# Graph layers on one core: where the second bisection bracket opens, who awaits the first layer step's stores, and the order in which the edge stage opens

## What is computed

```python
def L0(X, S):                                  # two steps s = 0, 1
    S = S + eye(n)
    Rf = S / S.sum(axis=1)[:, None]; Rb = S / S.sum(axis=0)[:, None]
    Xf, Xb, Xa, Z = X, X, X, 0
    for s in range(2):
        logits = (Xa @ W1) @ W2 @ (Xa @ W3).T
        # per row: keep the largest entries whose softmax adds up to 0.9, softmax over these
        A = nucleus(logits, 0.9)
        Xf, Xb, Xa = Rf @ Xf, Rb @ Xb, A @ Xa
        Z = Z + Xf @ U1[s] + Xb @ U2[s] + Xa @ U3[s]
    return layernorm(X + Z) * gamma + beta

def L1(x, adj):                                # the edge stage
    node_att = softmax(x @ node_w, axis=0)
    h = x @ edge_w
    e = where(adj > 0, h @ h.T, NEG_BIG)
    return adj * (node_att * softmax(e, axis=1)) @ (x @ weight) + bias

h = relu(layernorm(x)); x = x + L0(h, adj)
h = relu(layernorm(x)); x = x + L1(h, adj)
```

## Time and profile before

| | |
|---|---|
| median of 3 runs | 3840.46 us |
| the profiled execution | 3846.29 us, span 3844.5 us, mean granted PE clock 0.888 |
| DVE busy | 3540.4 us (92%) |
| ACT busy | 3104.4 us (81%) |
| PE busy | 3004.2 us (78%), weight load 2102.5 us |
| POOL busy | 358.5 us (9%) |
| first layer step, from its first to its last row | 54.95 to 1604.38 us |
| second layer step | 1609.59 to 3140.8 us |
| edge stage | from 3297.82 us |

### The profile page before, as it was taken

The page is one execution under the profiler, slowest core; times in us unless marked ns, Lnnn a source line. Parts: engine busy times, 40 slices in busy tenths (PEclk is TensorE's granted clock), DMA queues, the critical chain, the costliest instruction groups (busy, mean ns, idle before and its releaser), DMA issues. The chain is left out here.

```text
span 3844.5 us, 41925 instructions
## 1 busy us (share of the span) xinstructions
PE 3004.2 (78%) x14148; PEld 2102.5 (55%) x14148; DVE 3540.4 (92%) x4636; ACT 3104.4 (81%) x4477; POOL 358.5 (9%) x417
## 2 busy tenths in 40 slices
PE   6568887787878776648978888796978536799999
PEld 4456666575656654414544545363544425577777
DVE  6999999999999999699999999999999969577776
ACT  6999999999999999399899999999999913233333
POOL 3000000000000000000000000000000017234443
PEclk9689889898988988869989999898989768899999
DMA  2112121222222220211111111111111025122221
GB/s 90 63 54 87 63 97 54 92 67 79 80 67 87 68 78 15 109 56 49 52 35 47 35 57 32 45 42 40 53 35 47 7 80 193 46 104 103 98 91 50
DMA packets 108904, 254.28 MB, mean 66 GB/s; under 512 B 11984, under 2 KB 47888, under 8 KB 105360
## 3 DMA queue, kind: packets, MB, share of 16 engines
q1 hardware_dynamic: 82768, 217.76, 17.6%
q10 hardware_dynamic: 25920, 33.83, 2.5%
HBM read 217.47 MB, written 34.08 MB: 65 GB/s over the span
## 5 line engine op out<-in xcount | busy, mean ns | idle before, releaser
L691 DVE SCALAR_TENSOR_TENSOR s_dump<-s_rows,s_mid 128x3327 bf16<-128x3327 f32 x608 | 2238.3, 3681 | 1.0 <-issue 0.6
L637 ACT ACTIVATE s_adump<-s_rows,s_mid 128x3327 int8<-128x3327 f32 x324 | 995.1, 3071 | 10.5
L643 ACT ACTIVATE s_adump<-s_rows,s_mid 128x3327 int8<-128x3327 f32 x324 | 990.8, 3058 | 0.0
L899 PE MATMUL bank<-x,s_slab 128*128 128x512 f32 x1352 | 629.3, 609 | 0.0
L876 PE MATMUL bank<-kh,qs 128*128 128x512 f16 (+1 forms) x364 | 146.4, 402 | 365.5 <-DVE s_rows L670 354.9
L899 PEld LDWEIGHTS bank<-x,s_slab 128*128 128x128 f32 x1352 | 265.4, 197 | 277.4 <-issue 265.6
L943 PE MATMUL bank<-hb,s_wT 128*128 128x256 f32 x1352 | 355.9, 408 | 70.7 <-ACT s_wT L515 70.7
L943 PE MATMUL bank<-xab,s_wT 128*128 128x256 f32 x1352 | 351.0, 405 | 71.8 <-ACT s_wT L515 71.6
L1334 ACT ACTIVATE e_wh<-bank 128x512 f16<-128x512 f32 (+1 forms) x182 | 102.4, 565 | 343.2 <-PE bank L1438 343.2
L932 PE MATMUL bank<-ident,s_rows 128*128 128x128 f32 x1352 | 229.7, 297 | 190.5 <-DVE s_rows L745 189.4
L899 PE MATMUL bank<-hb,s_slab 128*128 128x257 f32 x1352 | 358.1, 407 | 0.0
(11 more groups left out here) (176 smaller groups left out, 4806.1 us busy)
## 6 DMA issues: line engine op xcount, KB each, us to landing
s_slab<-adjT_dram SPq DMA_DIRECT2D x104, 448.0 KB, 3.9
e_adj<-adjR_dram SPq DMA_DIRECT2D x26, 1664.0 KB, 7.0
s_slab<-adjT_dram SPq DMA_DIRECT2D x104, 384.0 KB, 3.7
strip<-adjR_dram SPq DMA_DIRECT2D x52, 448.0 KB, 3.5
strip<-adjR_dram SPq DMA_DIRECT2D x52, 384.0 KB, 3.3
su_d<-s_su_out ACTq DMA_DIRECT2D x26, 256.0 KB, 2.0
zu_d<-s_zu_out ACTq DMA_DIRECT2D x26, 256.0 KB, 2.0
sx_d<-s_sx_out ACTq DMA_DIRECT2D x26, 256.0 KB, 2.0
```

Of the source, the lines that this page charges most:

```text
L637: nc.scalar.activation(adump[:], row(g, r), ACT.Sign, bias=st(mid, g, 2), accum_out=cnt[:]).then_inc(S["a_eval"], 1)
L643: nc.scalar.activation(adump[:], row(g, r), ACT.Relu, bias=st(mid, g, 2), accum_out=gap[:]).then_inc(S["a_eval"], 1)
L691: nc.vector.scalar_tensor_tensor(out=dump[:], in0=row(g, r), scalar=st(mid, g, r), in1=row(g, r), op0=ALU.is_gt, op1=ALU.mult, accum_out=s ...
L899: ins = nc.tensor.matmul(acc, slab[:, i % NSLAB, j - PIECES[p], :], s_op[:, j, 0:SN], start=False, stop=(j == NT - 1))
```

## The change

Four edits in one kernel.

1. In `layer_step`, `begin(g, 1)` no longer stands ahead of the first pass of role 0 but between its `judge` and the first pass of role 1, in each of the groups 0 to 7 of both steps.
2. The three semaphores of the stores belong to the level above the first step (`kept_in`), are not cleared behind it, and ACT doesn't wait for them at its end. In the second step SP waits for them ahead of its first load, and DVE ahead of its memset. POOL's clears behind the first step become 49.
3. In `phase_edges`, `penalty(1)` stands behind `penalty(0)`, ahead of the first takes.
4. DVE's multiplication of row 0 by the adjacency stands behind the third take of row 1 (`EARLY = 3`), not ahead of the first.

```diff
@@ program
             later = [sb0(n, [P, NPAD], F16) for n in ("qs1", "kh1", "kl1")]
+            kept_in = {n: l0.enter_context(nc.semaphore("s0_" + n)) for n in ("xt_stored", "su_stored", "zu_stored")}
@@ layer_step
+            S.update(env["kept_in"])
...
             if s == 1:
+                for n in ("xt_stored", "su_stored", "zu_stored"):
+                    sp.wait_ge(env["kept_in"][n], 16 * NT)
                 for p in range(NPIECE):
...
-            if s == 0:
-                for n in ("xt_stored", "su_stored", "zu_stored"):
-                    act.wait_ge(S[n], 16 * NT)
-            else:
+            if s == 1:
                 act.wait_ge(S["sx_stored"], 16 * NT)
...
+            if s == 1:
+                for n in ("xt_stored", "su_stored", "zu_stored"):
+                    dve.wait_ge(env["kept_in"][n], 16 * NT)
             nc.vector.memset(rows[:, :, N:NPAD], 0.0).then_inc(S["rows_zero"], 1)
...
             for g in range(LAST):
-                for r in range(2):
-                    begin(g, r)
+                begin(g, 0)
                 for it in range(BISECT):
                     for r in range(2):
+                        if it == 0 and r == 1:
+                            begin(g, 1)
                         evaluate(g, it, r)
@@ phase_edges
+    EARLY = 3
...
             penalty(0)
+            penalty(1)
             dve.wait_ge(na["cut"], 1)
...
             nc.vector.tensor_scalar(col[:, 2:3], col[:, 1:2], -1.0, None, ALU.mult).then_inc(na["shift"], 1)
-            penalty(1)
-            dve.wait_ge(S["exp_done"], 1)
-            nc.vector.tensor_tensor(em[:, 0], em[:, 0], adj[:, 0], ALU.mult).then_inc(S["w_ready"], 1)
             for ch in range(NCH):
+                if ch == EARLY:
+                    dve.wait_ge(S["exp_done"], 1)
+                    nc.vector.tensor_tensor(em[:, 0], em[:, 0], adj[:, 0], ALU.mult).then_inc(S["w_ready"], 1)
                 take(1, ch)
             highest(1)
```

More of the change, by code:

```diff
@@ L405, in layer_step @@
             S.update({n: sem(tag + n) for n in (
-                "col_done", "csum_done", "rsum_ready", "rinv_ready", "turned", "xt_ready", "xt_stored", "su_done", "su_taken", "su_stored",
-                "zu_done", "zu_taken", "zu_stored", "qk_done", "k_high", "q_high", "qk_low", "q_kept")})
+                "col_done", "csum_done", "rsum_ready", "rinv_ready", "turned", "xt_ready", "su_done", "su_taken",
+                "zu_done", "zu_taken", "qk_done", "k_high", "q_high", "qk_low", "q_kept")})
         else:
```

## The result

The changed kernel takes 3831.22 us (median of 14 runs, 3828.26 to 3835.75), the kernel before 3841.47 us (14 runs, 3840.18 to 3843.55). The ratio is 0.9972, 95% interval 0.9965 to 0.9979: 10.8 us less by the ratio, with an interval of 8 to 13 us. The forecast was 3831.1 us, by a sum of 9.4 us.

The account below looks back on a forecast made before the run. DVE bounds the layer steps, PE the edge stage. Bracket 2.7, stores 1.0 and edges 5.7 sum to 9.4 us off the profiled 3846.29, less 5.8 to the runs' median: 3831.1 us, range 3827.5 to 3834.5.

Parts of the forecast that it names:

- The bracket: Layer steps, role 1's opening moved: two waits saved (6.40 us), pair's price 3.84 lost, 0.14 back at heads; net +2.7 us.
- 16 prices of 0.24: Layer steps: in all 16 groups the pair between judge and second pass costs 0.24 us, 3.84 us lost in total.
- The rival that the pair is nearly free: Layer steps: the pair costs only 0.12 us, so the bracket gives 4.6 us and the time is 3829.2; chance 0.15.
- what the sum would have been by the sentence of the Trainium skill: Layer steps: with no extra semaphore cost, the bracket's sum would be its upper bound, +4.6 us instead of +2.7.
- The stores: Boundary between the layer steps: store wait and three clears leave DVE's gap, +1.0 us, between 0.5 and 1.4.
- The rival that the boundary doesn't hang on the store: Boundary between the steps: only three clears go and three waits come, time 3832.1 us; chance 0.05.
- The edges: Edge stage's opening: row 1's maximum starts 5.7 us earlier and everything behind shifts with it; bounds 4.8 to 6.6.
- my upper bound: Edge stage's opening: if PE returns at the high clock and stays there, the gain is 6.6 us.
- The rival in which the penalty isn't made up: Edges, row 0: the penalty's 1.8 us are lost, sum 7.6, time 3832.9; chance 0.16 together with a take-over loss.
- The rival of a long stretch at the lower clock: Edge stage: a 60 us stretch at granted clock 0.58 would cost PE 25 us, time 3856; chance 0.04.

Follow-up runs that it names:

- the price alone: Kernel before, with role 1's opening moved behind the judge in groups 1 to 7 only, group 0 as before: 3843.61 us, ratio 1.0003.
- few_clears: Changed kernel, with semaphores of first stage, first layer step and edge stage never cleared, their clear blocks and barriers left out: 3820.33 us, ratio 0.9949.
- third_penalty: Changed kernel plus role 1's opening ahead of role 0's judge, those three stages' clears dropped, third penalty row behind row 1's second take: 3816.13 us.
- b_only: Kernel before, with the edit of the stores alone: 3841.64 us, ratio 0.9997.
- takes_only: Kernel before, with three takes ahead of the edges' multiplication, second penalty left behind row 0's maximum: 3837.59 us, ratio 0.999.

## Why the prediction was right

**The bracket.** All steps held: the first passes start 3.2 us earlier, the second passes 0.37 us behind the judge, ACT follows at the take-over because PE, and so ACT, hung on DVE's `qs` instruction (PE restarts 0.44 us behind its start in both kernels, and the wait at the take-over stayed 0.97 us), and 1.5 and 1.4 us per step arrive at the ninth group. Forecast +2.7, by the stamps +2.9. The forecast counted 16 prices of 0.24; the one of the fourth group was not paid. The rival that the pair is nearly free falls by the changed kernel's own stamps, and the price alone shows it again without the gain. With it falls what the sum would have been by the sentence of the Trainium skill, VectorE: DVE Perf Modes, section The DRAIN you can't avoid, that "the semaphore costs nothing extra here". For these instructions of 0.14 us the trace doesn't agree with it: the next one starts 0.06 us later if it needs nothing of them (241.86, 241.92), and 0.18 if it does (241.44, 241.62). No run here tests it for long instructions.

What the forecast didn't have is that a part of that price in the second step may be no loss. DVE waits there for PE's logits in the middle of some groups: 3.0 us before, 3.2, 2.8, 2.4, 2.1, 1.8, 1.6, 1.4 and 1.0 us in the eight other traces without the pair behind the judge, and 0, 0, 0.4 and 1.7 us in the four with it. Where DVE would have waited anyway, being later costs nothing. These waits also differ between kernels that are alike there, so how much of the difference is the pair's and how much is PE's clock stays open.

**The stores.** Forecast +1.0 (0.5 to 1.4), measured 0.8: 4.47 to 4.49 us in four traces, against 5.29. The trace also holds POOL's clears themselves, which the views leave out, and they divide the gap. From DVE's last end to the first clear it was 0.95 us and is 0.25; from there to the last clear's end 3.95 and 3.74; from there to the memset 0.39 and 0.50. So the store was worth 0.7 us, three clears 0.2, and the three waits ahead of the memset cost 0.1. The rival that the boundary doesn't hang on the store falls by the first of the three.

The size of one part was off: I took a clear at 0.06 us from gaps with 25 and 30 of them, and for 49 that line gives 3.85 us where the gap is 4.48. A clear starts 0.071 us behind the one before it, at every boundary. But in the row of 49, as in the 52 of before, one of them starts 0.36 us behind the one before it, 0.3 us late. That pause, 0.2 us from the clear's size and the 0.1 us of the waits make up the difference. What causes the pause no run shows; without the clears of the first two boundaries it stands among the 30 ahead of the edge stage, whose gap is 3.02 us there.

**The edges.** Forecast +5.7 (4.8 to 6.6), measured 5.4 by the changed kernel's trace, but by two errors that cancel. I let PE come back at the lower clock for the third chunk; it came back at the higher one after 1.94 us of idling, and again after 2.80, so row 1's maximum gained my upper bound, 6.6. And I let everything behind it shift unchanged; PE's next restart fell into a longer stretch at the lower clock than before, and that gave back 1.2 us. That the two nearly cancel is luck. The traces with both edits, without few_clears and third_penalty, need 45.5, 45.5, 47.6, 47.6 and 47.7 us from memset to row 2's maximum, those without either edit 52.8 to 53.4. The term is thus 5 to 8 us, by where the lower clock fell. In few_clears the granted clock was at the lower level until 5.7 us behind the memset (3.0 to 3.2 us in the other five), row 0's maximum came 1 us later than in the others, two more such stretches followed, and it needed 50.1. The rival in which the penalty isn't made up falls: row 0's maximum came 0.06 us later, not 1.8. The rival of a long stretch at the lower clock didn't happen: 1.00 from 3338 us on.

**The sum** of what the change did by its own places is 9.1 us, forecast 9.4, measured by the ratio 10.8 (8 to 13). That the forecast time, 3831.1 us, meets the median within 0.1 us is luck in part: it starts from the median of three runs, 3840.46, and the longer series has 3841.47 for the same kernel.

## What to carry to other kernels

A wait taken off one place by moving an instruction is paid at each place to which it is moved: count its repetitions, and look for a spot where it stands under another wait (here, ahead of the judge instead of behind it, the same two instructions went from 0.24 us to nothing). When two profiled executions differ by more than the change can explain, make a ledger by stamps over the whole span first; more than a third of this difference lay in a stage that the change doesn't touch and in waits that it wasn't made for. And where a barrier's gap is made of semaphore clears, moving a wait out of its way gains little until the clears go.

## What the runs showed of the hardware

- A semaphore clear on POOL starts 0.071 us behind the one before it, and DVE stands still for all of them: its gap at a boundary is 2.39 us with 25 clears and 2.73 us with 30, and 4.48 us with 49, among them one pause of 0.3 us. Without the clears and their block it is 0.36 us.
- On DVE an instruction of one column (0.14 us) lets the next one start 0.06 us later if that needs nothing of it, and 0.18 us later if that waits for its result. The judge, which waits for a pass's accumulator, starts 0.12 us behind the accumulator's read, and two independent small instructions fit in between (241.86 to 241.98).
- In the opening of the edge stage PE came back from 1.94 us of idling at the higher level (2.4 GHz) in all seven traces that have it. From 2.80 us it came back at the higher level in five traces and at the lower (1.2 GHz) in few_clears; from 3.27 us at the lower in nine (in b_only the clock fell with the first matmul) and at the higher in takes_only; from 3.94 us, in takes_only again, at the higher:

```profile
3305.98 1.03 PE L1441 MATMUL bank<-hth 128*128 128x512 f16 x2 [2.80 <-DVE e_rows L1372]
```
```profile
3309.79 0.60 PE L1430 MATMUL bank<-hth 128*128 128x512 f16 x2 [3.94 <-DVE e_rows L1361]
```

  The length of the idle time alone doesn't tell the level.
- One kernel's runs spread over 2 to 11 us. Between the traces (one for each kernel) many of DVE's stretches repeat within 0.1 us, as the 461.2 to 461.3 us from row 2's maximum to the last one's. What differs where no edit reaches are the stretches that end with PE's serial chains: 27.6 to 29.2 us for the tail of the first step, 173.6 to 178.1 us from the second step's last cut to the edges.
